# An MLP on products of split parts, and normalisations and expert weighting as two-input operations

## The chip, the core and the metric

The kernel runs on one core of a Trainium2 chip. The metric is the device time of one execution in microseconds; a version is run several times and its median is taken. The engines are PE (TensorE), DVE (VectorE), ACT (ScalarE), POOL (GpSimd) and the DMA queues of SP and ACT.

## The reference

A transformer block with self attention, cross attention and an MLP, then a router with three experts over evidence from the context, for 32 sequences of 128 tokens with 128 channels, all in float32. Cut to what matters:

```python
# B=32 sequences, N=128 tokens, H=128; S=128 tokens of context; 16 heads of 8; MLP = 512; E = 3 experts of 256
def L0(x, c, context, ...):
    shift_a, scale_a, gate_a, shift_m, scale_m, gate_m = split(silu(c) @ W_mod + b_mod, 6)
    x = x + gate_a * (attention(modulate(ln(x), shift_a, scale_a)) @ W_proj + b_proj)      # self
    x = x + attention(ln(x) @ W_qc + b_qc, ln(context) @ W_kvc + b_kvc) @ W_cproj + b_cproj  # cross
    x_norm2 = modulate(ln(x), shift_m, scale_m)            # ln(x) * (1 + scale_m) + shift_m
    h = gelu(x_norm2 @ W_mlp1 + b_mlp1)                    # [.., 512]
    return x + gate_m * (h @ W_mlp2 + b_mlp2)
def L1(x, anchor, bank, ...):                              # bank = the context
    nx = ln(x) * gamma + beta
    evidence = softmax((nx @ Wq) @ (bank @ Wk).T / sqrt(H)) @ (bank @ Wv)
    combined = concat(nx, evidence, anchor)
    p = softmax(combined @ router_W + router_b)            # 3 experts
    routed = sum_e p_e * (silu(combined @ e_w1[e] + e_b1[e]) @ e_w2[e] + e_b2[e])
    g = sigmoid(silu(combined @ gate_w1 + gate_b1) @ gate_w2 + gate_b2)
    return x + g * (routed @ out_w + out_b)
```

## The kernel before, in words

The 32 sequences are 8 groups (`NG`) of 4 (`GB`), a group's tile is 128 x 512 (`GT`). The first 325 us are attention, in rounds of an order written out by hand: `round_steps` gives each step a time, and every engine goes through the same list and does its own part of each step; `attention_events` turns it into events. The last attention round also derives the router's weights (`derive`) and, on POOL, takes the router's weights apart into a high part, rounded to the format fp32r, and a rest (`split_weights`, which calls `split`, lines 656 to 661). Its first steps of the MLP are the events of round `NG`, then `between_cores` and `rest_of_groups` go on: each engine runs the steps of `MLP_STEPS` for i = 2, 3, 4 alone and for i = 5, 6, 7 mixed with the first steps of the router (`ROUTER_STEPS`), then the router's groups.

One group g of the MLP goes through these steps, and an entry `(name, lag, k)` does it for group i + lag:

- `stats` (L806 to L812 on DVE, L648 and L650 on POOL): mean and variance, then the inverse deviation `rstd` as a power on POOL. `norm` (L820, DVE): `(x - mean) * rstd` into `m_XN`, four instructions of 128 x 128, each with mean and rstd as one value per token.
- `xt` (PE, L975): four transposes of `m_XN` into PSUM. `xt_read` (ACT, L725): four reads with scale and shift into `m_XT`.
- `first` (PE, L939): W_mlp1's chunk k (of 4) times `m_XT`, in float32; the trace shows two matmul records for one such product. `gelu` (ACT, L713) reads the bank into `m_H[:, k]`.
- `second` (PE): W_mlp2's chunk k times `m_H[:, k]`, all four into one bank, for the group before. `gate` (DVE, L835) reads that bank into `YT`; `turn_back` (PE) transposes it back, and DVE adds it to `X` (L841).

Engines are strictly in order: what stands behind a wait in an engine's list waits too. `m_XT`, `m_XN` and each chunk of `m_H` have one buffer, the FIRST and SECOND banks two each. In the router, `hidden` already works with split parts: for each weight and each input it makes three products (high by high, high by rest, rest by high) with `r_WNS`, `r_US`, `r_NXS`, `r_EVS`; the inputs are taken apart by `split` on POOL. `expert` (DVE, L914 to L920) adds biases (`r_T`) and weights three experts into `r_R`.

## Time and profile before

| | |
|---|---|
| median of 3 runs | 578.65 us (576.69 to 580.65) |
| the profiled execution | 576.7 us, of which its span is 574.9 us |
| PE, PEld busy | 541.4 us (94%), 382.1 us (66%) |
| DVE, ACT, POOL busy | 424.2 us (74%), 384.0 us (67%), 271.3 us (47%) |
| mean granted clock of TensorE | 0.993 of 2.4 GHz |

All times of rows are of the profiled execution, counted from the start of its span. A row of a timeline gives start, length, engine, line, operation, output and inputs (buffer numbers left out; PS is PSUM) and count; behind it, in brackets, the idle time of the engine and what ended it. PE is the matmul part of TensorE and PEld its loading of weights. The ends of matmuls are modelled, so that the distance from one start to the next is the surer price.

### The profile page before, as it was taken

What the parts mean: (1) busy time and instruction counts of PE and PEld (TensorE: products, weight loads), DVE (VectorE), ACT (ScalarE), POOL (GpSimd) and SP (SyncE); (2) the same over time, 40 slices, a digit from 0 to 9 for tenths busy, and PEclk for the clock granted to TensorE, in tenths of its full rate; (3) what the DMA queues carried; (4) which work ended last, traced back from release to release, by engine and by line L of the source; (5) the groups of instructions that cost most, each with busy time, mean ns of one, the idle gap of its engine ahead of it and who ended that gap; (6) DMA issues with size and microseconds to landing.
All of it is one profiled execution on the core that took longest, in us unless ns stands there. A gap on an engine that the chain in (4) does not pass through costs nothing.

```text
span 574.9 us, 16422 instructions
## 1 busy us (share of the span) xinstructions
PE 541.4 (94%) x6177; PEld 382.1 (66%) x6177; DVE 424.2 (74%) x1255; ACT 384.0 (67%) x897; POOL 271.3 (47%) x294
## 2 busy tenths in 40 slices
PE   6988999999999999999999989997999999999995
PEld 5745665566666666666667534454788788788895
DVE  4788988888899798989787534556586786786565
ACT  6547687677777778787776655464754854854862
POOL 5638769399494878888903210124034034034000
PEclk9999999899999999999999899999999999999999
DMA  4765656344153543344400010000001001000000
GB/s 130 159 170 132 176 149 150 78 114 124 45 133 91 133 117 96 89 107 117 114 5 3 2 36 0 2 1 19 0 20 39 20 19 36 18 18 20 19 20 18
DMA packets 48716, 39.38 MB, mean 69 GB/s; under 512 B 6241, under 2 KB 48002, under 8 KB 48642
## 3 DMA queue, kind: packets, MB, share of 16 engines
q1 hardware_dynamic: 46568, 34.62, 23.3%
q10 hardware_dynamic: 2074, 3.77, 2.3%
q8 instruction: 47, 0.77, 0.6%
q14 instruction: 27, 0.22, 0.1%
HBM read 10.06 MB, written 2.10 MB: 21 GB/s over the span
## 4 chain that ended last, share of the span: by engine, by line
PE 64%; DVE 11%; POOL 7%; DMA 5%; ACT 4%; SPq 4%; issue 3%; ACTq 0%; DVEq 0%; POOLq 0%
PE PS L939 35%; PE PS L1808 6%; PE PS L1774 5%; PE PS L975 3%; SPq L1322 3%; PE PS L1860 3%; DVE NM L1590 3%; PE PS L1872 3%; DMA Qs<-MT 2%; PE PS L1792 2%; PE PS L1830 2%; PE PS L1865 2%; DMA Ks<-Kp 1%; POOL rstd L1368 1%; POOL rest L1399 1%
## 5 line engine op out<-in xcount | busy, mean ns | idle before, releaser
L1590 DVE TENSOR_REDUCE NM<-PS 128x4 f32<-128x512 f32 x256 | 163.4, 682 | 30.9 <-PE PS L1774 30.3
L1476 ACT ACTIVATE PR<-PS 128x512 f32<-128x512 f32 x256 | 139.7, 600 | 28.1 <-PE PS L1792 27.4
L1774 PEld LDWEIGHTS PS<-Ks,Qs 64*128 64x128 bf16 x1024 | 57.3, 94 | 53.4 <-DVE NM L1590 29.3
L1774 PE MATMUL PS<-Ks,Qs 64*128 64x128 bf16 x1024 | 83.6, 218 | 5.8 <-DVE NM L1590 3.8
L1792 PE MATMUL PS<-Qs,Ks 64*128 64x128 bf16 x1024 | 83.7, 219 | 4.5 <-DMA Qs<-MT 3.9
L1808 PE MATMUL PS<-PR,Va 128*32 128x128 f32 x2048 | 83.1, 280 | 0.0
L733 ACT ACTIVATE r_HID<-PS,ANC 128x128 f32<-128x128 f32 x224 | 63.0, 380 | 19.4 <-PE PS L939 19.3
L648 POOL TENSOR_TENSOR m_veps<-m_mv,m_eps 128x4 f32<-128x4 f32 x16 | 3.2, 201 | 143.0 <-DVE m_mv L812 143.0
L1792 PEld LDWEIGHTS PS<-Qs,Ks 64*128 64x128 bf16 x1024 | 57.1, 94 | 8.3 <-DMA Qs<-MT 4.4
L1808 PEld LDWEIGHTS PS<-PR,Va 128*32 128x32 f32 x2048 | 48.5, 109 | 20.9 <-issue 6.0
L939 PE MATMUL PS<-r_NXS,r_WNS 128*128 128x512 f32 x168 | 53.1, 424 | 0.0
L939 PE MATMUL PS<-WO,r_HID 128*128 128x128 f32 x384 | 47.7, 278 | 0.2
L939 PE MATMUL PS<-r_EVS,r_US 128*128 128x512 f32 x168 | 47.7, 392 | 0.0
L939 PEld LDWEIGHTS PS<-WO,r_HID 128*128 128x128 f32 x384 | 44.6, 192 | 1.6 <-DVE r_T L914 1.3
L1860 PE MATMUL PS<-XT,W 128*128 128x512 f32 x64 | 34.9, 633 | 1.9 <-ACT XT L1512 1.4
L939 PEld LDWEIGHTS PS<-r_EVS,r_US 128*128 128x128 f32 x168 | 31.5, 188 | 7.2
L939 PEld LDWEIGHTS PS<-r_NXS,r_WNS 128*128 128x128 f32 x168 | 29.5, 189 | 7.7 <-issue 3.4
L713 ACT ACTIVATE m_H<-PS,V 128x512 f32<-128x512 f32 x32 | 21.3, 692 | 19.8 <-PE PS L939 19.8
L939 PE MATMUL PS<-m_XT,W 128*128 128x512 f32 x64 | 32.0, 600 | 0.3 <-ACT m_XT L725 0.3
L939 PE MATMUL PS<-m_H,W 128*128 128x512 f32 x64 | 31.5, 592 | 0.0
L762 ACT ACTIVATE r_GTH<-r_GS 128x512 f32<-128x512 f32 x8 | 5.0, 631 | 38.7 <-DVE r_GS L907 38.7
L659 POOL TENSOR_TENSOR r_EVS<-r_EV,zeros 128x512 fp32r<-128x512 f32 x8 | 8.3, 1039 | 47.5 <-DVE r_EV L888 47.5
(197 smaller groups left out, 1103.6 us busy)
## 6 DMA issues: line engine op xcount, KB each, us to landing
Qs<-Qp SPq DMA_DIRECT2D x96, 128.0 KB
Ks<-Kp SPq DMA_DIRECT2D x90, 128.0 KB
CTXG<-in_ctx SPq DMA_DIRECT2D x8, 256.0 KB, 3.6
r_CTX<-in_ctx SPq DMA_DIRECT2D x8, 256.0 KB, 2.9
out<-X SPq DMA_DIRECT2D x8, 256.0 KB, 2.3
X<-in_x SPq DMA_DIRECT2D x7, 256.0 KB, 4.4
W<-in_weights ACTq DMA_DIRECT2D x2, 855.0 KB
Qs<-MT SPq DMA_DIRECT2D x62, 8.0 KB
```

What stands on the lines that cost most here:

```text
L713: nc.scalar.activation(H[:, k, :], FIRST_BANK[k % 2][:, :], ACT.Gelu_apprx_tanh, bias=vec("bmlp1", k))\
L733: last = nc.scalar.activation(HID[:, k, b * P:(b + 1) * P], HIDDEN_BANK[k % 3][:, b * P:(b + 1) * P], ACT.Silu, bias=ANC[:, k, bass.ds(g * ...
L939: return nc.tensor.matmul(to, lhsT, rhs, start=start, stop=stop)
L975: last = nc.tensor.transpose(bank[:, b * P:(b + 1) * P], source(b), ident[:, :])
L1322: sp.dma_start(to, source).then_inc(stacked[k], 16)
L1476: nc.scalar.activation(PR[:, u, :], T_BANK[u % 2][:, :], ACT.Exp, scale=SCALE)\
L1590: nc.vector.tensor_reduce(out=NM[:, c.b // 2, c.second, u // 2, u % 2 * 4:u % 2 * 4 + 4, 0], in_=S_BANK[score_bank(c, u)[0]][:, :].rearran ...
L1774: last = nc.tensor.matmul(S_BANK[bank][:, j * P:(j + 1) * P], Qs[c.stack][rows, lo + j, cols], Ks[c.stack][rows, lo + j, cols], start=True ...
L1792: last = nc.tensor.matmul(T_BANK[u % 2][:, j * P:(j + 1) * P], Ks[c.stack][rows, lo + j, cols], Qs[c.stack][rows, lo + j, cols], start=Tru ...
L1808: last = nc.tensor.matmul(O_BANK[p.turn][TW * j:TW * j + TW, at:at + P], Va[c.mem][:, c.b, 4 * (u // 2) + j, u % 2 * TW // 2:u % 2 * TW // ...
L1860: last = nc.tensor.matmul(PS[fill_bank(name, g)][:, :], w(WEIGHT[name[0]][kind]), source(name, g)[:, :], start=True, stop=True)
L1872: last = nc.tensor.matmul(GROUP_BANK[:, :], w(("proj", "cproj")[KIND[name]]), OgT[KIND[name]][:, :], start=True, stop=True)
```

## The change

- *Products of the MLP.* `m_W1S` and `m_W2S` hold the high part and the rest of W_mlp1 and W_mlp2; POOL makes them in the last attention round with `split` (the same two operations as for the router's weights), behind a wait for the score steps that used the memory under them. The stacks `Qs` and `Ks` are laid out in another order for that.
- *The input.* A new step `xt_parts` on DVE copies `m_XT` into the high part of `m_XTS` (two buffers) and subtracts it from `m_XT` for the rest. `xt_read` now comes right behind `xt` in `MLP_STEPS`, with `xt_parts` behind it.
- *The hidden values.* Behind each gelu, ACT waits for it and copies `m_H[:, k]` into the high part of `m_HS`; POOL subtracts for the rest. `second` waits for the rest.
- *PE* makes three products of split parts for each `first` and each `second`, where it made one in float32. It also waits for the weights' parts.
- *Two-input forms.* `normalise` (MLP and router) becomes `scalar_tensor_tensor` with rstd as a broadcast second tensor; the first expert's weighting (`r_R`, L917) becomes `tensor_tensor` with a broadcast second tensor.
- Four semaphores of the attention are used again, with their counts carried on.

Hunk headers keep the line numbers; context is cut. `split` is the function at line 656.

```diff
@@ -243,7 +243,7 @@
...
                  + fill_steps(31.0, "mlp_xt", 0, (0, 31.1))
-                 + [(t, "split", "weights", k, 0) for k, t in enumerate((2.5, 6.0, 22.5, 24.5))]
+                 + [(t, "split", "weights", k, 0) for k, t in enumerate((2.5, 6.0, 9.0, 12.0, 22.5, 24.5))]
                  + mlp_steps(21.2, "stats", 0) + mlp_steps(23.4, "norm", 0)
@@ -256,7 +256,7 @@
...
                  + mlp_steps(8.43, "second", 0, 3) + mlp_steps(8.44, "norm", 3) + mlp_steps(8.45, "first", 1, 2)
-                 + mlp_steps(8.46, "first", 1, 3) + mlp_steps(8.47, "xt_read", 2) + mlp_steps(8.48, "gelu", 1, 2)
+                 + mlp_steps(8.46, "first", 1, 3) + mlp_steps(8.35, "xt_read", 2) + mlp_steps(8.36, "xt_parts", 2) + mlp_steps(5.11, "xt_parts", 1) + mlp_steps(8.48, "gelu", 1, 2)
                  + mlp_steps(8.49, "gelu", 1, 3) + mlp_steps(8.5, "gate", 0))
@@ -381,9 +381,9 @@
...
 MLP_STEPS = (
-    ("stats", 2, 0), ("xt", 1, 0),
+    ("stats", 2, 0), ("xt", 1, 0), ("xt_read", 1, 0), ("xt_parts", 1, 0),
     ("first", 0, 0), ("second", -1, 0), ("first", 0, 1), ("second", -1, 1),
-    ("turn_back", -2, 0), ("norm", 2, 0), ("first", 0, 2), ("first", 0, 3), ("xt_read", 1, 0),
+    ("turn_back", -2, 0), ("norm", 2, 0), ("first", 0, 2), ("first", 0, 3),
     ("second", -1, 2), ("gelu", 0, 2), ("second", -1, 3), ("gelu", 0, 3), ("gate", -1, 0),
@@ -458,7 +458,8 @@
...
 def mlp_and_router(nc, stack, X, V, ctxin, w, vec, rows1, condT, mod, gbm, half, zeros, YT, ident, PS, load_w2, out,
-                   bank_filled, bank_read, max_done, exp_done, o_normed, o_stored):
+                   bank_filled, bank_read, shifted_done, max_done, exp_done, o_normed, o_stored,
+                   high_ready, low_ready):
@@ -530,6 +531,10 @@
...
     D = rb("r_D", [P, GT])
+    W1S = rb("m_W1S", [P, 2, 4 * P], F32R)
+    W2S = rb("m_W2S", [P, 2, 4 * P], F32R)
+    XTS = [rb(f"m_XTS{k}", [P, 2, GT], F32R) for k in range(2)]
+    HS = rb("m_HS", [P, 2, 4, GT], F32R)
@@ -553,6 +558,8 @@
...
     bank_filled["mlp_xt"], bank_read["mlp_xt"] = xt_turned, xt_read
+
+    xt_high, xt_split, h_high, h_split = (high_ready["k0"], low_ready["k0"], high_ready["q0"], low_ready["q0"])
     masked = sem("masked")
@@ -652,6 +659,9 @@
...
                 inverse_deviation(0, g)
+            elif name == "first" and k < 2 or name == "gelu":
+                pool.wait_ge(h_high, 4 * g + (NG + k + 1))
+                nc.gpsimd.tensor_tensor(HS[:, 1, k, :], H[:, k, :], HS[:, 0, k, :], ALU.subtract).then_inc(h_split, 1)
@@ -679,8 +689,13 @@
...
                 pool.wait_ge(load_w2, 80)
-            elif k > 1:
-                pool.wait_ge(bank_read["derive"], DERIVED.index(("u_low", "u_high")[k - 2]) + 1)
+            elif k in (2, 3):
+
+                pool.wait_ge(shifted_done, 16 * (2 * NG - 2))
+                to, source = ((W1S, w("mlp1")), (W2S, w("mlp2")))[k - 2]
+                return split(to, source, (weights_high, k + 1), weights_split)
+            elif k > 3:
+                pool.wait_ge(bank_read["derive"], DERIVED.index(("u_low", "u_high")[k - 4]) + 1)
             to, source = (WNS, w("e_nx", lo, hi - lo)) if k < 2 else (US, U[:, lo:hi])
@@ -709,9 +724,13 @@
...
             if later(g):
-                act.wait_ge(second_done, 4 * g + (k - 3))
+                act.wait_ge(h_split, 4 * g + (NG + k - 3))
             nc.scalar.activation(H[:, k, :], FIRST_BANK[k % 2][:, :], ACT.Gelu_apprx_tanh, bias=vec("bmlp1", k))\
                 .then_inc(gelu_done, 1)
+            act.wait_ge(gelu_done, 4 * g + (k + 1))
+            if later(g):
+                act.wait_ge(second_done, 4 * g + (k - 3))
+            nc.scalar.activation(HS[:, 0, k, :], H[:, k, :], ACT.Copy).then_inc(h_high, 1)
@@ -719,7 +738,7 @@
...
                 if later(g):
-                    act.wait_ge(first_done, 4 * g)
+                    act.wait_ge(xt_split, g + NG)
                 for b in range(GB):
@@ -817,8 +836,8 @@
...
             for b in range(GB):
-                last = nc.vector.tensor_scalar(to[:, b * P:(b + 1) * P], x_batch(g, b), mv[:, s, b, 0:1],
-                                               rstd[:, s, b:b + 1], ALU.subtract, ALU.mult)
+                last = nc.vector.scalar_tensor_tensor(to[:, b * P:(b + 1) * P], x_batch(g, b), mv[:, s, b, 0:1],
+                                                      rstd[:, s, b:b + 1].to_broadcast([P, P]), ALU.subtract, ALU.mult)
             last.then_inc(d_norm[s], 1)
@@ -826,6 +845,17 @@
...
                 normalise(0, g, XN, xt_turned)
+            elif name == "xt_parts":
+                dve.wait_ge(xt_read, g + 1)
+                if g > 1:
+                    dve.wait_ge(first_done, 4 * (g - 1))
+                elif g == 1:
+                    dve.wait_ge(exp_done, 4 * NCORE)
+                else:
+                    dve.wait_ge(shifted_done, 16 * (2 * NG - 2))
+                nc.vector.tensor_copy(XTS[par][:, 0, :], XT[:, :]).then_inc(xt_high, 1)
+                dve.wait_ge(xt_high, g + (NG + 1))
+                nc.vector.tensor_tensor(XTS[par][:, 1, :], XT[:, :], XTS[par][:, 0, :], ALU.subtract).then_inc(xt_split, 1)
             elif name == "gate":
@@ -914,7 +944,7 @@
...
                 dve.wait_ge(expert_read, GB * g + (b + 1))
-                nc.vector.tensor_scalar(R[:, b, :], t[:, 0:P], RP[:, b, 0:1], None, ALU.mult).then_inc(routed, 1)
+                nc.vector.tensor_tensor(R[:, b, :], t[:, 0:P], RP[:, b, 0:1].to_broadcast([P, P]), ALU.mult).then_inc(routed, 1)
                 for e in range(1, NE):
@@ -985,17 +1015,23 @@
...
                     pe.wait_ge(exp_done, 4 * NCORE)
+                    pe.wait_ge(weights_split, 4)
                 if k == 0:
-                    pe.wait_ge(xt_read, g + 1)
+                    pe.wait_ge(xt_split, g + (NG + 1))
                 if k > 1 or later(g):
                     pe.wait_ge(gelu_done, 4 * g + (k - 1))
-                product(FIRST_BANK[k % 2][:, :], w("mlp1", k * P, P), XT[:, :]).then_inc(first_done, 1)
+                chunk = slice(k * P, (k + 1) * P)
+                product(FIRST_BANK[k % 2][:, :], W1S[:, 0, chunk], XTS[par][:, 0, :], True, False)
+                product(FIRST_BANK[k % 2][:, :], W1S[:, 0, chunk], XTS[par][:, 1, :], False, False)
+                product(FIRST_BANK[k % 2][:, :], W1S[:, 1, chunk], XTS[par][:, 0, :], False, True).then_inc(first_done, 1)
             elif name == "second":
...
                     pe.wait_ge(x_added, g - 1)
-                pe.wait_ge(gelu_done, 4 * g + (k + 1))
-                product(SECOND_BANK[par][:, :], w("mlp2", k * P, P), H[:, k, :], start=k == 0, stop=k == 3)\
-                    .then_inc(second_done, 1)
+                pe.wait_ge(h_split, 4 * g + (NG + k + 1))
+                chunk = slice(k * P, (k + 1) * P)
+                product(SECOND_BANK[par][:, :], W2S[:, 0, chunk], HS[:, 0, k, :], k == 0, False)
+                product(SECOND_BANK[par][:, :], W2S[:, 0, chunk], HS[:, 1, k, :], False, False)
+                product(SECOND_BANK[par][:, :], W2S[:, 1, chunk], HS[:, 0, k, :], False, k == 3).then_inc(second_done, 1)
             elif name == "turn_back":
@@ -1088,7 +1124,7 @@
...
-            pe.wait_ge(weights_split, 2 * -(-NHC * P // GT))
+            pe.wait_ge(weights_split, 2 * -(-NHC * P // GT) + 2)
             pe.wait_ge(xt_read, NG)
@@ -1192,7 +1228,7 @@
...
             nc, stack, X, V, ctxin, w, vec, rows1, condT, mod, gbm, half, zeros, YT, ident, PS, load_w2, out,
-            bank_filled, bank_read, max_done, exp_done, o_normed, o_stored)
+            bank_filled, bank_read, shifted_done, max_done, exp_done, o_normed, o_stored, high_ready, low_ready)
@@ -1205,8 +1241,6 @@
...
         rest = sb("rest", [P, 2, GT])
-        Qs = [sb(f"Qs{k}", [P, NJ, GT], BF16) for k in range(STACKS)]
-        Ks = [sb(f"Ks{k}", [P, NJ, GT], BF16) for k in range(STACKS)]
         zrow = sb("zrow", [32, GT], BF16)
@@ -1217,6 +1251,9 @@
...
         On = sb("On", [P, 2, 2 * P])
+        Qs, Ks = [None] * STACKS, [None] * STACKS
+        for k in (1, 0, 2):
+            Qs[k], Ks[k] = (sb(f"{what}s{k}", [P, NJ, GT], BF16) for what in "QK")
         OgT = [sb(f"OgT{k}", [P, GT]) for k in range(2)]
@@ -1369,6 +1406,8 @@
...
                     extra["split"](ev[2])
+                elif ev[:2] == ("read", "mlp_xt"):
+                    extra["mlp"]("xt_parts", 0, 0, 0, 0)
                 elif ev[:2] == ("init", "third"):
@@ -1716,6 +1755,8 @@
...
                     extra["derive"](DERIVED[ev[2]], ev[3])
+                elif ev[:2] == ("read", "mlp_xt"):
+                    extra["mlp"]("xt_parts", 0, 0, 0, 0)
                 elif name == "read" and ev[1] in ("yt_s", "yt_c"):
```

## Rows read from the trace of the kernel before

**Rows 1.** Chain of waits, 325 to 404 us: share of each line.

```profile
by line: PE PS L939 69.0%; PE PS L975 11.2%; ACT m_XT L725 5.5%; issue 3.3%; ACT m_H L713 2.0%; ACT r_E L744 1.9%; ACT L744 1.6%; PE PS L1872 1.4%; ACT L713 1.2%; DVE r_EV L888 0.9%; ACT r_CTXT L738 0.6%; PE PS L1830 0.6%; PE PS L1876 0.6%;
```

**Rows 2.** Windows: length, busy of PE, PEld, DVE, ACT, POOL; clock, DMA, GB/s.

```profile
325.80:342.15 16.35, 13.71 (x44) 6.59 (x44) 7.76 (x38) 9.75 (x20) 2.41 (x4) 1.00 0.12 33
...
350.35:358.50 8.15, 8.12 (x24) 3.77 (x25) 4.30 (x18) 4.03 (x9) 1.20 (x2) 1.00 0.00 0
...
366.65:375.90 9.25, 9.24 (x30) 4.70 (x31) 6.16 (x29) 5.20 (x11) 2.16 (x4) 1.00 0.00 1
```

**Rows 3.** Timeline of PE in the MLP: start, us, what, count.

```profile
363.03 1.88 PE L939 MATMUL PS<-m_XT,W 128*128 128x512 f32 x4
364.75 1.88 PE L939 MATMUL PS<-m_H,W 128*128 128x512 f32 x4
```

**Rows 4.** Timeline of PE in the router, products of split parts.

```profile
553.84 0.85 PE L939 MATMUL PS<-r_NXS,r_WNS 128*128 128x512 f32 x3
554.52 0.84 PE L939 MATMUL PS<-r_EVS,r_US 128*128 128x512 f32 x3
```

**Rows 5.** ACT: timeline of one group; last, the Tanh's line (ns min/median/max).

```profile
352.98 0.69 ACT L713 ACTIVATE m_H<-PS,V 128x512 f32<-128x512 f32 x1 [1.62 <-PE PS L939]
...
356.86 1.50 ACT L725 ACTIVATE m_XT<-PS,mod 128x128 f32<-128x128 f32 x4 [1.47 <-PE PS L939]
...
L762 ACT ACTIVATE r_GTH<-r_GS x8: 629/630/632, 424.3 to 566.0; 128x512 f32<-128x512 f32 x8
```

**Rows 6.** Timeline of DVE in the same group.

```profile
350.36 1.37 DVE L835 TENSOR_SCALAR YT<-PS,mod,gbm 128x128 f32<-128x128 f32 x4 [1.72 <-PE PS L939]
351.64 0.86 DVE L806 BATCH_NORM_STATS2 m_stat<-X 128x6 f32<-128x128 f32 x4
...
352.61 0.37 DVE L812 BATCH_NORM_AGGREGATE m_mv<-m_stat 128x2 f32<-128x6 f32 x4
355.08 0.69 DVE L841 TENSOR_TENSOR X<-PS,X 128x512 f32<-128x512 f32 x1 [2.09 <-PE PS L975]
355.69 1.11 DVE L820 TENSOR_SCALAR m_XN<-X,m_mv,m_rstd 128x128 f32<-128x128 f32 x4
```

**Rows 7.** Timelines of POOL and DVE, 311 to 317 us.

```profile
311.25 0.20 POOL L648 TENSOR_TENSOR m_veps<-m_mv,m_eps 128x4 f32<-128x4 f32 x1 [23.71 <-DVE m_mv L812]
...
312.52 1.04 POOL L659 TENSOR_TENSOR r_US<-U,zeros 128x512 fp32r<-128x512 f32 x1
313.63 1.27 POOL L661 TENSOR_TENSOR r_US<-U,r_US 128x512 fp32r<-128x512 f32 x1
...
312.58 4.27 DVE L820 TENSOR_SCALAR m_XN<-X,m_mv,m_rstd 128x128 f32<-128x128 f32 x4 [1.41 <-POOL m_rstd L650]
```

**Rows 8.** Timelines of POOL and DVE at 16 and at 400 us.

```profile
15.86 1.22 POOL L1403 TENSOR_TENSOR Kp<-rest,Kp 128x512 bf16<-128x512 f32 x1
...
16.09 1.53 DVE L1715 TENSOR_TENSOR Qp<-rest,Qp 128x512 bf16<-128x512 f32 x1
...
399.28 1.04 POOL L659 TENSOR_TENSOR r_NXS<-r_NX,zeros 128x512 fp32r<-128x512 f32 x1
...
399.79 0.56 DVE L900 TENSOR_TENSOR r_LS<-r_LG,r_lmax 128x12 f32<-128x12 f32 x1
400.27 1.36 DVE L835 TENSOR_SCALAR YT<-PS,mod,gbm 128x128 f32<-128x128 f32 x4
```

**Rows 9.** r_R: line of its scalar form (ns), timeline of DVE, waits of PE.

```profile
L917 DVE TENSOR_SCALAR r_R<-r_T,r_RP x32: 285/286/1028, 421.0 to 569.6; 128x128 f32<-128x128 f32 x32
...
443.51 0.74 DVE L920 SCALAR_TENSOR_TENSOR r_R<-r_T,r_RP,r_R 128x128 f32<-128x128 f32 x2
...
PEld PS L939 <- DVE r_T L914: 1.3, 6, 0.3
```

**Rows 10.** Windows around an idle PE, columns as in Rows 2.

```profile
316.60:317.50 0.90, 0.07 (x2) 0.00 (x0) 0.90 (x4) 0.90 (x3) 0.17 (x1) 0.87 0.00 0
317.50:318.50 1.00, 0.97 (x1) 0.50 (x2) 0.96 (x7) 0.26 (x1) 0.00 (x0) 0.50 0.00 0
```

## The prediction

> **What bounds the kernel now.** I read the windows by stretch first, to find the stage that the change touches: the MLP of eight groups runs from 325.8 to 404.1 us, and the router behind it. The chain of waits inside that stage [rows 1] is 69% matrix products of line 939, 11% transposes, and only 5.5% ACT's read of XT: TensorE sets the pace. The reader should see in [rows 2] that one pure MLP group takes 8.15 us with PE busy 8.12 of them, while DVE works 4.30, ACT 4.03 and POOL 1.21. PE's own timeline [rows 3] gives the price of a product: four matmuls are issued in 1.72 us (363.03 to 364.75), so one product (two records) holds PE for 0.86; eight products are 6.88, the two sets of four transposes about 0.44 each. The products of split parts that the router already has [rows 4] start 0.68 us apart for three (553.84 to 554.52), so a product costs 0.68.
>
> **The change, part by part.**
> (a) Products. 8 groups x 8 products x (0.86 - 0.68) = 11.5 us less on PE; per group 1.44. That is the whole possible gain, and only as long as PE stays last.
> (b) ACT. Each gelu (0.69) gets a Copy of 128x512 behind it, which waits for the gelu itself. The trace has no such SBUF-to-SBUF copy; the nearest row is the Tanh from SBUF, 0.63, so I take 0.60 (bounds 0.53, if its start overlaps the work before it, and 0.69). ACT per group: XT read 1.38 net of overlap, four times 0.69+0.03+0.60 = 5.28, sum 6.7 [rows 5]; a copy also waits for the `second` product of the group before, about 0.4 once per group: 7.1. So ACT becomes the bound near 7.1 us if nothing else waits.
> (c) POOL. Four subtracts per group. The nearest row, the low half of `split`, is 1.27 [rows 7], so 5.1 a group, beside the inverse deviation, 1.27 (311.25 to 312.52): 6.3.
> (d) DVE. Now [rows 6]: gate 1.37, statistics 1.34 (351.64 to the end of the averages, 352.61 + 0.37), x addition 0.69, normalise 1.11, 4.30 with little else. Added: copy 0.42 (bounds 0.35 and 0.69; estimates from half and all of the 0.69 that one 128x512 operation takes) and subtract 0.69. Normalise as a two-input form: 4 x 0.32 = 1.3, because two of the two-input r_R operations take 0.74 together, and the scalar form 0.286 [rows 9]; about 6.0 in all without waits.
> (e) The lock between DVE and POOL, which decides the case. At 312.58 four normalise operations took 4.27 us instead of 1.11 [rows 7]: POOL was busy without a pause, and each DVE operation came through only as one POOL operation ended, one for one, and POOL's own rows follow each other with next to no gap (312.52 + 1.04, then 313.63). The question is whether the two-input form escapes this. [Rows 8] say no: the TENSOR_TENSOR of 16.09, both inputs in SBUF, took 1.53 against the 0.69 of [rows 6]; POOL's operation ended at 17.08 and the DVE one 0.54 later, so it did all its work behind POOL's. The one of 399.79, with 12 elements a partition, took 0.56 and ended 0.03 behind POOL's (399.28 + 1.04). Operations of DVE that read PSUM are not held (YT at 400.27: four in 1.36, as at 350.36, with POOL at work beside it). So the change puts 5.1 us of POOL reads per group beside six DVE operations that must wait for them: copy, subtract, and four normalises.
>
> Walk through one locked group, time 0 where the last normalise of group g+1 ends: transposes, ACT starts at 0.72; XT read to 2.1; gelu 2.8; copy 3.4; POOL could subtract at 3.5. DVE meanwhile did the gate (to 1.3) and statistics (to 2.6), so POOL, in order, is at the inverse deviation until 4.0, and the subtracts start there. DVE: copy and subtract of XT from 2.6 to 3.8 (4.6 if the inverse deviation's pow on POOL holds it), x addition to 4.4 or more: the first normalise meets the first subtract. All four pass behind the four subtracts: 4.0 + 4 x 1.3 + 0.15 = 9.4, and 9.8 with the end of the XT subtract behind the pow. If one of the four slips in ahead: 8.0. So a group takes 8.0 to 9.8 against 8.15; I take the middle, 8.98.
>
> The sum, in stages.
> *Start* (325.8 to 342.15): `first` of group 0 waits for copy and subtract, +1.1; cheaper products and the earlier XT read give back about 3; the normalise of group 3 behind four subtracts of group 1 is +4.1; the XT subtract or one normalise more behind a POOL operation is +0.3 to +2.6. Together +2.5 to +4.8, I take +3.7.
> *Three pure groups* to 366.65 (the iterations that start at 342.15, 350.35 and 358.50): -0.4 to +5.0, I take +2.5.
> *Mixed stage*, 366.65 to 404.1, of which the first iteration took 9.25: PE saves up to 0.18 x 24 = -4.3. Against it, the two router normalises queue behind subtracts (+1.5 to +4), of ACT's 8 copies (4.8) around two loads of a table and the exps I let half show (+2.4), and the last `second` has copy 0.60 and subtract 1.27 in front of it, perhaps a router split of 2.3 as well (+1.9 to +4.2). Together +1.5 to +6.3; these waits overlap in part, so I take +3.2.
> *Router*: its r_R operation waits for POOL in some groups (up to 1.03 against 0.29) and will go on waiting; PE's waits for r_T total 1.3 us [rows 9], so nothing above that could be won. In the last group, four times 0.07 (half of 0.74, less 0.286, rounded down) lie on the path: +0.3.
> *Splits of W1 and W2*, two at about 2.3: free, they fall into POOL's idle time of 23.71 us before 311.25 [rows 7]; without that cover they would cost 4.6. Their wait counts 224 of the 256 shifted score steps, which are complete as the last attention round starts. PE's wait for them is met long before 325. The reuse of semaphores and the new order of buffers cost nothing that a row shows. The stall at 312.58 stays: the same operations, +0.07.
> Sum: 3.7 + 2.5 + 3.2 + 0.3 = +9.7 us (bounds +3.9 and +16.4). The profiled execution was 576.7, 1.8 more than its span, and the median of the three runs 1.95 above it: 578.65 + 9.7 = 588.4.
>
> The Trainium skill bears on (e): its page "SBUF — State Buffer", section "Who interferes with whom", says that a Vector instruction with two SBUF inputs also contends with a GpSimd instruction that reads SBUF, that the pair is held for the whole instruction, and that whoever comes first blocks the other. The waits of DVE agree (1.53 and 0.56 above). By the second half POOL would lose DVE's data time as well, an estimate of 0.27 + 0.53 a group from that page's rule; the trace shows POOL's next operation starting 0.07 behind its last at 313.63 although DVE had just come through, so the sum has no such term; by the rule it would be up to 6 us more.
>
> **The rivals.**
> *No lock* (the other sign): the form with a broadcast second operand does not wait, or POOL's pauses let it through. Then ACT sets 7.1 us per group: start -1.9, three groups -3.2, mixed stage -0.4, in all -5.5: 573.1. For it: the work of every engine is under 7.1. Against it: [rows 8]. If even ACT's copies were hidden, PE's 11.5 would be the limit, 567. It decides from the point where the four normalises take under about 2.5 us.
> *Mild lock*: the phases of DVE and POOL settle so that one or two normalises wait, -2 to +4: 579.5. A group of 8.0 is this side's end.
> *The clock*: in a locked group PE is idle about 3 us in 9.8. An idle PE of 0.86 us at 316.6 was followed by a granted clock of 0.50 in the next stretch [rows 10], the lower level of 1.2 GHz, while in 325.80 to 342.15 PE was idle for 2.64 us in all and the clock stayed at 1.00 [rows 2]. At the lower level the eight products need 10.9 us, more than the group. If that happens in half of the groups, +8 on top of the forecast: 596.
>
> **How the numbers follow.** About 1% is what a measurement of this kernel can tell. Chances: forecast (+3.9 to +16.4) 0.58, clock 0.10, mild lock 0.15, no lock 0.17. Faster by over 1% needs -5.8: the better half of no lock, 0.09. Within 1%: the rest of it, mild lock, and the forecast's lowest edge, 0.28. Slower: 0.63. The range leaves out the best of no lock and the worst of the clock: 573 to 598.
>
> **What would show it.** Right: the product's starts 0.68 apart; normalise m_XN over 3 us per group, each operation ending as a POOL subtract ends; PE waiting for m_XN's transposes; a group of 8 to 10 us; the MLP 7 to 13 us longer. Wrong: normalise at 1.3 us per group, ACT near full and a group near 7.1 (no lock), or a PEclk row under 9 in that stage (clock). The forecast is too high if the XT copy and subtract regularly come before the subtracts of POOL, and too low if POOL is delayed in its turn.

## The result, and the profile after

Three executions of the changed kernel took 588.1, 588.5 and 590.9 us, beside a median of 579.2 us (576.7 to 580.7) for the kernel before: the ratio on record is 1.0214, 95% interval 1.0156 to 1.0272, some 12 us; the two medians alone give 9.3 us. A fourth execution was in a slow state (1223.8 us, at a granted clock of 1.000, without a trace that could say why) and is not in these numbers; with it the median would be 589.7. The profiled execution took 588.5 us, its span 586.7, where that of the kernel before had 574.9.

The page of the kernel after, first the busy times, the slices of PE and its clock, and the chain that ended last:

```profile
PE 536.3 (91%) x6241; PEld 398.3 (68%) x6241; DVE 452.8 (77%) x1271; ACT 403.2 (69%) x929; POOL 319.6 (54%) x330
...
PE   7988999999999999999998776876999999999995
...
PEclk9999999999999999999999989787999999999998
...
PE 55%; DVE 18%; POOL 10%; issue 5%; DMA 5%; SPq 4%; ACT 3%; ACTq 0%; DVEq 0%; POOLq 0%
...
L664 POOL TENSOR_TENSOR m_HS<-m_H,m_HS 128x512 fp32r<-128x512 f32 x32 | 41.4, 1312 | 18.2 <-ACT m_HS L733 18.1
```

PE has holes in slices 22 to 28 (308 to 411 us), nearly all of them in the MLP, and its clock row falls to 7 and 8 there. The chain inside that stage (318 to 416 us) answers to [rows 1]: products of the MLP were 69% of it; now line 969 has under a third, and the normalisation, a line that did not appear before, has 13.5%:

```profile
by line: PE PS L969 31.8%; DVE m_XN L839 13.5%; issue 10.9%; PE PS L1005 8.2%; POOL m_HS L664 5.1%; DVE r_XN L839 3.1%; POOL m_rstd L657 2.6%; DVE m_XTS L858 2.4%; DVE YT L865 2.4%; DVE m_stat L825 1.6%; DVE m_XTS L856 1.5%; ACT m_H L728 1.
```

The windows between the transposes of successive groups have the columns of [rows 2], whose pure group was 8.15 us with PE busy for 8.12:

```profile
330.47:340.75 10.28, 5.22 (x27) 4.16 (x27) 8.18 (x17) 6.34 (x12) 8.04 (x7) 0.97 0.17 51
340.75:348.77 8.02, 7.92 (x33) 6.33 (x33) 6.14 (x21) 5.42 (x11) 3.95 (x4) 0.82 0.00 0
348.77:358.70 9.93, 6.79 (x32) 5.10 (x32) 9.60 (x21) 7.38 (x14) 9.50 (x8) 1.00 0.01 3
358.70:368.39 9.69, 6.62 (x33) 5.21 (x33) 9.23 (x21) 6.36 (x12) 6.85 (x6) 0.95 0.00 0
368.39:378.92 10.53, 10.53 (x38) 8.31 (x39) 6.96 (x25) 6.58 (x13) 3.93 (x4) 0.72 0.00 1
```

Two kinds of group take turns. In three of the five PE works 5.2 to 6.8 us and DVE 8.2 to 9.6: DVE is last. In the other two (8.02 and 10.53) PE is busy nearly to the end, at a mean clock of 0.82 and 0.72 of 2.4 GHz, that is, for a part of the time at the lower level of 1.2. The timeline of the third window shows what DVE does:

```profile
351.84 0.69 DVE L858 TENSOR_TENSOR m_XTS<-m_XT,m_XTS 128x512 fp32r<-128x512 f32 x1
351.94 1.46 POOL L657 TENSOR_TENSOR m_rstd<-m_veps,half 128x4 f32<-128x4 f32 x1
...
353.38 5.13 POOL L664 TENSOR_TENSOR m_HS<-m_H,m_HS 128x512 fp32r<-128x512 f32 x4
353.44 5.21 DVE L839 SCALAR_TENSOR_TENSOR m_XN<-X,m_mv,m_rstd 128x128 f32<-128x128 f32 x4
...
358.70 0.66 PE L1005 MATMUL PS<-ident,m_XN 128*128 128x128 f32 x4 [3.14 <-DVE m_XN L839]
```

Four normalisations took 5.21 us, as four subtractions beside them took 5.13; each of the four ended 0.15 us behind the end of a subtraction, and PE stood idle for 3.14 us until the last was done. In [rows 7] this was a single stall at 312.58. Now it comes in full in three more of the eight groups (5.16, 5.21 and 5.12 us); in the other four the normalisations took 1.1 to 2.2 us, so that none or one of them waited.

To see where the time went I cut every execution at the same four marks: the first transpose of group 0 (line 1005), those of groups 3 and 6, and the first product of the router's hidden layer. The first column is the time of the first mark. Start, pure groups, mixed stage and router are the distances between them and to the end, in us; the kernels of the experiments are in the same table.

```
kernel          attention  start   pure  mixed  router  | ratio to before, 95%
before             323.3    18.9   24.5   37.5   170.8  |
after              318.2    22.5   27.6   47.5   170.8  | 1.0214 1.0156-1.0272
before_layout      322.7    18.9   24.5   37.5   170.9  | 0.9961 0.9933-0.9989
one_input          323.4    22.2   27.4   44.8   170.4  | 1.0194 1.0137-1.0252
pe_filler          318.1    22.5   27.6   43.2   170.8  | 1.0185 1.0153-1.0216
rest_dve           322.2    24.8   23.2   43.7   170.8  | 1.0150 1.0100-1.0201
halves             320.6    22.9   23.8   43.1   170.8  | 1.0140 1.0106-1.0174
second_only        320.5    18.8   24.2   44.4   170.8  | 1.0087 1.0056-1.0117
norm_in_two        316.2    21.0   24.4   44.7   170.8  | 1.0081 1.0050-1.0113
no_rest            318.8    18.5   21.7   41.2   170.8  | 0.9971 0.9942-1.0001
first_load         321.1    23.3   27.2   42.6   171.2  | 1.0203 1.0151-1.0256
first_only         322.1    16.4   21.3   35.9   171.2  | 0.9871 0.9843-0.9899
half_second        322.0    17.7   20.5   38.1   170.9  | 0.9868 0.9824-0.9912
first_one          318.7    16.4   21.3   35.9   170.8  | 0.9825 0.9785-0.9865
```

Between the two profiled executions the MLP grew by 16.8 us (3.6 + 3.2 + 10.0), the router by nothing, and the attention stage, in which no instruction was to become faster, was 5.1 us shorter.

### The profile page after: what moved, and what is told of

Same layout as the page of the kernel before. It is cut to its first block, busy times and chain, and to the rows that moved or that the text cites. A ratio compares the mean times of both kernels' runs of the same rounds, so it can differ in the third digit from the quotient of the medians.

```text
span 586.7 us, 16671 instructions
## 1 busy us (share of the span) xinstructions
PE 536.3 (91%) x6241; PEld 398.3 (68%) x6241; DVE 452.8 (77%) x1271; ACT 403.2 (69%) x929; POOL 319.6 (54%) x330
## 4 chain that ended last, share of the span: by engine, by line
PE 55%; DVE 18%; POOL 10%; issue 5%; DMA 5%; SPq 4%; ACT 3%; ACTq 0%; DVEq 0%; POOLq 0%
PE PS L969 27%; PE PS L1849 6%; PE PS L1815 5%; DVE m_XN L839 3%; PE PS L1005 3%; PE PS L1901 3%; DVE NM L1629 3%; SPq L1359 3%; DMA Qs<-MT 2%; PE PS L1833 2%; PE PS L1913 2%; PE PS L1871 2%; PE PS L1906 2%; DVE r_T L944 1%; DMA Ks<-Kp 1%
## 5 line engine op out<-in xcount | busy, mean ns | idle before, releaser
L664 POOL TENSOR_TENSOR m_HS<-m_H,m_HS 128x512 fp32r<-128x512 f32 x32 | 41.4, 1312 | 18.2 <-ACT m_HS L733 18.1
L969 PE MATMUL PS<-m_XTS,m_W1S 128*128 128x512 f32 x96 | 31.8, 458 | 1.5 <-DVE m_XTS L858 1.5
L1402 POOL TENSOR_TENSOR veps<-mv,eps 128x4 f32<-128x4 f32 x24 | 4.9, 203 | 47.0 <-DVE mv L1694 47.0
```

Source lines behind the costliest of these rows:

```text
L664: nc.gpsimd.tensor_tensor(HS[:, 1, k, :], H[:, k, :], HS[:, 0, k, :], ALU.subtract).then_inc(h_split, 1)
L969: return nc.tensor.matmul(to, lhsT, rhs, start=start, stop=stop)
```

## The experiments

**1. The subtractions left out.** no_rest keeps POOL's subtraction for group 0 alone:

```diff
-            elif name == "first" and k < 2 or name == "gelu":
+            elif g == 0 and (name == "first" and k < 2 or name == "gelu"):
                 pool.wait_ge(h_high, 4 * g + (NG + k + 1))
...
-                pe.wait_ge(h_split, 4 * g + (NG + k + 1))
+                pe.wait_ge(h_high if g else h_split, 4 * g + (NG + k + 1))
```

> The changed kernel, with POOL's subtraction of the rests of the gelu outputs left out from the second group on: the middle product of each second MLP product then reads the rests of group 0, so its part of the output is wrong by the size of a rest. TensorE's 24 products a group, ACT's copies and DVE's parts stay. Theory A (the subtractions, in turn with DVE's normalisations and parts, set the length of a group): the groups fall from about 10 us to 7.2 to 7.8 us, and the time to 572 to 577 us. Rival B (ACT's copies, or the longer chain gelu, copy, second product): the copies remain, groups of over 9 us, 586 us or more. Rival C (TensorE at half its clock in this stretch costs the time): nothing here changes what the clock depends on in a known way, so 586 to 590 us with the same low clock.

It took 574.5 us beside 575.7: its ratio is 2.4% under the changed kernel's, some 14 us. That is in theory A's range, and not in that of B or C. But the cut also takes the subtraction out of the chain from the gelu to the second product, and out of what the next gelu waits for. And the clock did not stay as it was: its mean was 0.979 to 0.992 here against 0.973 to 0.979, so a part of the 14 us can be the clock's. It is no clear gain over the kernel before (the interval reaches 1.0001): the three pure groups took 6.4, 7.6 and 7.6 us, and in the last two PE, though it has less work, waits again:

```profile
351.34:358.96 7.62, 6.97 (x33) 5.26 (x32) 5.35 (x20) 6.36 (x13) 1.21 (x2) 1.00 0.00 0
```

**2. One of the two products at a time.** first_only takes the second product back to fp32, with the gelu output as before and nothing on ACT or POOL; second_only does the opposite. The core of first_only:

```diff
-                nc.gpsimd.tensor_tensor(HS[:, 1, k, :], H[:, k, :], HS[:, 0, k, :], ALU.subtract).then_inc(h_split, 1)
...
-            nc.scalar.activation(HS[:, 0, k, :], H[:, k, :], ACT.Copy).then_inc(h_high, 1)
...
-                product(SECOND_BANK[par][:, :], W2S[:, 0, chunk], HS[:, 0, k, :], k == 0, False)
-                product(SECOND_BANK[par][:, :], W2S[:, 0, chunk], HS[:, 1, k, :], False, False)
-                product(SECOND_BANK[par][:, :], W2S[:, 1, chunk], HS[:, 0, k, :], False, k == 3).then_inc(second_done, 1)
+                product(SECOND_BANK[par][:, :], w("mlp2", k * P, P), H[:, k, :], start=k == 0, stop=k == 3)\
+                    .then_inc(second_done, 1)
```

> The changed kernel, with the second MLP product back to fp32 from the gelu output: no copies on ACT, no subtractions on POOL; the first product still of split parts. Theory A: TensorE saves 4 x (0.86 - 0.68) = 0.7 us in each of 8 groups against the kernel before, and nothing waits for POOL; the start, where the parts have to be made before the first product, costs some 1 to 2 us: 573 to 577 us. Rival D (the longer chain from transpose over ACT and two DVE operations to the first product costs more than the products save, whatever POOL does): 580 to 585 us.

> The changed kernel, with the first MLP product back to fp32 from the transposed normalised x: no parts on DVE; the second product still of split parts, with ACT's copies and POOL's subtractions. Theory A: the four normalisations still go in turn with the four subtractions, but the two operations for the parts and their waits are gone: groups of 8.2 to 9.2 us, 580 to 585 us. Rival D (the chain for the parts costs the time): 574 to 578 us. Rival B (ACT's copies and the chain behind the gelu): 586 us or more.

568.8 us and 581.0 us: the first split alone is 1.3% faster than the kernel before, 4 us better than theory A's range had it; the second alone is 0.9% slower, within theory A's range, though its pure groups (8.4, 7.7 and 8.2 us) are at or under the foot of the 8.2 to 9.2 expected. The window of a pure group of first_only has PE busy to the end again:

```profile
352.64:359.74 7.10, 7.10 (x29) 4.51 (x28) 5.33 (x20) 4.05 (x9) 1.75 (x2) 1.00 0.00 0
```

That is 1.05 us under the 8.15 of before, where the four cheaper products give only 0.72; nearly all of the other 0.33 stands at the two sets of four transposes, which took 0.58 and 0.44 us from their start to the next start before, and 0.36 each here; why they cost less is not shown. Rival D falls: the longer chain to the first product is hidden.

**3. The load alone.** first_load is first_only with POOL's four subtractions a group put back, of constant data into a tile that nobody reads; nobody waits for them (the edit is shown against first_only):

```diff
+            elif name == "first" and k < 2 or name == "gelu":
+                pool.wait_ge(gelu_done, 4 * g + (k + 1))
+                nc.gpsimd.tensor_tensor(HS[:, 1, k, :], w("mlp2"), W2S[:, 0, :], ALU.subtract)
```

> The kernel first_only (only the first product of split parts; 7.10 us a group, TensorE without a gap) with a load on POOL that nobody needs: at each gelu one subtraction of 128x512 of constant data into a tile that nobody reads, four a group. No wait of any other engine is added, and ACT and TensorE do what they did. Theory A (POOL's subtractions hold up DVE's operations with two SBUF inputs one for one): DVE's 5.3 us a group grow by 2 to 4 us of waits, past TensorE's 7.1: groups of 8 to 9.5 us and 575 to 586 us. Rival B (POOL costs only through the chain gelu, copy, rest, second product): 567 to 571 us, as without the load.

587.5 us beside first_only's 568.8: +18.6 us, for work that no instruction waits for, a little more than theory A's range had. This is the cleanest of the runs: no engine waits for the new work. The one thing that could queue behind it is POOL's own inverse deviation, and DVE's wait for that grew by 0.9 us only (the last numbers of the two rows below). So what is left is what POOL's reads do to DVE, and what follows from that; the lower clock follows as well, in this profile with up to 5.5 of the 18.6 us (an estimate: half of the time that PE worked at 1.2 GHz in the MLP; none in first_only). The groups of lines of DVE in 323 to 400 us, first_only and then first_load:

```profile
L832 DVE SCALAR_TENSOR_TENSOR m_XN<-X,m_mv,m_rstd 128x128 f32<-128x128 f32 x28 | 7.9, 346 | 0.9 <-POOL m_rstd L657 0.9
```

```profile
L835 DVE SCALAR_TENSOR_TENSOR m_XN<-X,m_mv,m_rstd 128x128 f32<-128x128 f32 x28 | 21.6, 831 | 1.8 <-POOL m_rstd L657 1.8
```

and the same group of the kernel after:

```profile
L839 DVE SCALAR_TENSOR_TENSOR m_XN<-X,m_mv,m_rstd 128x128 f32<-128x128 f32 x24 | 21.6, 957 | 1.2 <-POOL m_rstd L657 1.1
```

In first_load 28 x (831 - 346) ns = 13.6 us are waits inside the normalisations, and in the changed kernel 24 x (957 - 346) ns = 14.7 us. PE's idle time in the MLP grew by 13.7 us from first_only to first_load.

**4. The size of what is waited for.** halves cuts each subtraction into two of 256 columns; norm_in_two does the four normalisations of a group of the MLP as two operations of 512 columns, the router's as before.

```diff
+                for lo in range(0, GT, GT // 2):
+                    part = slice(lo, lo + GT // 2)
+                    last = nc.gpsimd.tensor_tensor(HS[:, 1, k, part], H[:, k, part], HS[:, 0, k, part], ALU.subtract)
+                last.then_inc(h_split, 1)
```

> The changed kernel, with each subtraction of 128x512 on POOL cut into two of 128x256. Theory A (a DVE operation with two inputs in SBUF gets through at the end of a POOL operation, one for one): a locked normalisation takes some 0.75 us in place of 1.3, so four of them 3 us in place of 5.2; a group becomes 1 to 2 us shorter, the time 577 to 584 us. If POOL's fixed cost eats the gain (two halves take over 1.7 us in place of 1.3), 585 to 590 us. Rivals B and C: no difference, 588 to 591 us; or longer, if only POOL's total matters.

```diff
+                nc.vector.tensor_tensor(t, x, mv[:, 0, :, 0:1].to_broadcast([P, GB, P]), ALU.subtract)\
+                    .then_inc(x_centred, 1)
+                dve.wait_ge(x_centred, g + 2)
+                nc.vector.tensor_tensor(t, t, rstd[:, 0, :].unsqueeze(2).to_broadcast([P, GB, P]), ALU.mult)\
+                    .then_inc(d_norm[0], 1)
```

> The changed kernel, with the four normalisations of 128x128 a group in two operations of 128x512 (x minus the mean, spread over the columns; then times the reciprocal deviation): about 1.4 us of DVE without waits, as before, but two operations that can meet a subtraction of POOL where there were four. Theory A (one wait for each operation, whatever its size): two locked operations take up to 2 x 1.35 us in place of 4 x 1.3, groups 1 to 2.5 us shorter: 574 to 581 us. If a longer operation waits longer, in proportion to its columns, no gain: 585 to 589 us.

584.0 us (the top of the expected range) and 581.3 us (just above it). The timelines, first of halves, then of norm_in_two:

```profile
356.44 3.70 POOL L666 TENSOR_TENSOR m_HS<-m_H,m_HS 128x256 fp32r<-128x256 f32 x5
356.50 3.05 DVE L842 SCALAR_TENSOR_TENSOR m_XN<-X,m_mv,m_rstd 128x128 f32<-128x128 f32 x4 [0.26 <-POOL m_rstd L657]
```

```profile
349.99 5.92 POOL L665 TENSOR_TENSOR m_HS<-m_H,m_HS 128x512 fp32r<-128x512 f32 x4
350.20 1.64 DVE L842 TENSOR_TENSOR m_XN<-X,m_mv 128x512 f32<-128x512 f32 x1
351.87 1.65 DVE L845 TENSOR_TENSOR m_XN<-m_XN,m_rstd 128x512 f32<-128x512 f32 x1
```

Behind POOL operations of half the size four normalisations take 3.05 us, not 5.21; as two operations they take 3.3. So a DVE operation waits once, for the POOL operation under way, at both of the sizes tried. The three pure groups fall by 3.9 and 3.3 us in sum. What the prediction left out shows in the second timeline: beside DVE's 512-column operations POOL's four subtractions take 5.92 us, not 5.13, because two of them take 1.73 each and not 1.3. POOL waits in its turn.

**5. The two-input forms undone.** one_input has tensor_scalar again for normalisation and first weighting.

```diff
-                last = nc.vector.scalar_tensor_tensor(to[:, b * P:(b + 1) * P], x_batch(g, b), mv[:, s, b, 0:1],
-                                                      rstd[:, s, b:b + 1].to_broadcast([P, P]), ALU.subtract, ALU.mult)
+                last = nc.vector.tensor_scalar(to[:, b * P:(b + 1) * P], x_batch(g, b), mv[:, s, b, 0:1],
+                                               rstd[:, s, b:b + 1], ALU.subtract, ALU.mult)
```

> The changed kernel, with the two-input forms undone: normalisations and the first expert weighting again as tensor_scalar. Theory A as the prediction has it (the old form waits for POOL's subtractions just as the new one does; without one beside it it takes 0.28 us in place of 0.34): 585 to 590 us. Rival E (only the new form waits): 573 to 580 us.

589.2 us, ratio 1.0194: no difference from the changed kernel that the intervals can tell. Rival E falls, since the old form waits as the new one does:

```profile
358.48 5.01 DVE L839 TENSOR_SCALAR m_XN<-X,m_mv,m_rstd 128x128 f32<-128x128 f32 x4 [0.19 <-POOL m_rstd L657]
```

**6. The rests on DVE.** rest_dve moves the four subtractions to DVE, at the same places of the order.

```diff
+        def h_rest(g, k):
+            dve.wait_ge(h_high, 4 * g + (NG + k + 1))
+            nc.vector.tensor_tensor(HS[:, 1, k, :], H[:, k, :], HS[:, 0, k, :], ALU.subtract).then_inc(h_split, 1)
...
+            if name == "first" and k < 2 or name == "gelu":
+                h_rest(g, k)
```

> The changed kernel, with the rests of the gelu outputs computed by DVE in place of POOL, at the same places of the order. DVE has 5.35 + 4 x 0.69 = 8.1 us of work a group and no operation of POOL beside it but the small ones. Theory A (the price is the meeting of the two engines, not the work): 8.1 to 9 us a group, 577 to 584 us, less than with POOL although DVE does more. Rival B (the chain behind the gelu sets the group; DVE now also stands waiting for ACT's copies): 588 us or more.

586.4 us: a miss for theory A's number, 2 us above its range. Its pure groups (8.2, 7.4 and 7.6 us) are as short as expected or shorter, and 4.4 us shorter in sum than with POOL. Two of them:

```profile
347.02:355.18 8.16, 6.57 (x32) 5.21 (x33) 7.81 (x25) 6.98 (x14) 1.75 (x2) 1.00 0.00 0
355.18:362.60 7.42, 6.57 (x32) 5.18 (x32) 7.35 (x25) 5.90 (x12) 1.68 (x2) 1.00 0.01 3
```

But the start (24.8 us) is longer than in any other kernel, and the mixed stage 6.2 us longer than before. In both TensorE worked for a part of the time at 1.2 GHz (mean clock 0.86 and 0.88, against 1.00 before), which makes up to 3.5 and 5.2 us of them (an estimate: length times what is missing from 1). In the whole time the two ways can't be told apart, as the intervals of 1.0150 and 1.0214 overlap: only the pure groups show that meeting POOL is dearer than DVE's extra work.

**7. The clock.** pe_filler gives TensorE ten spare products in each of groups 3 to 7, ahead of the wait in which it was idle.

```diff
+                if g > 2:
+                    for _ in range(10):
+                        product(SCORE_BANK[1][:, :], W1S[:, 0, 0:P], W1S[:, 0, :])
                 pe.wait_ge(d_norm[0], g + 1)
```

> The changed kernel, with ten further products of split weights (128x512, 0.23 us each, 2.3 us in all) ahead of the wait for the normalised x, in groups 3 to 7, into a PSUM bank that nobody reads: there TensorE stood idle for 3 to 5 us in most of these groups. In the profile of the changed kernel TensorE was granted half the clock for some 20 us of the MLP stage, and two stretches with TensorE busy throughout lay in it (8.0 us at 0.82 with 7.92 busy, 10.5 us at 0.72 with 10.53 busy). Theory H (idle time made by the waits is followed by half clock, and that costs a part of the time, 3 to 8 us): with less idle time the clock stays up and the time is 581 to 587 us although TensorE does more. Theory A alone (what DVE waits for POOL sets the groups, and the clock costs nothing beside it): 588 to 596 us, since the fillers take up to 5 x 2.3 us and are hidden only where TensorE waited.

588.1 us, ratio 1.0185, at the lowest edge of theory A's range and just above theory H's. The mean granted clock of its six executions is 0.983 to 0.993, that of the changed kernel 0.973 to 0.979: it rose in all of them, and the time fell by 0.3%, less than the intervals can tell. In the profiled execution, the fastest of the six, two middle groups are:

```profile
350.88:359.54 8.66, 8.66 (x43) 7.16 (x42) 6.45 (x21) 6.36 (x12) 6.35 (x7) 1.00 0.00 1
359.54:368.21 8.67, 8.67 (x43) 7.16 (x42) 6.52 (x21) 6.36 (x12) 6.35 (x7) 1.00 0.00 0
```

Its three pure groups are as long in sum as those of the changed kernel (27.6 us), with 2.3 us more work of PE in each; its mixed stage is 4.2 us shorter, with 2.3 us of fillers in it. This is no clean test of the clock, for two reasons. PE is now busy throughout the pure groups, so the fillers are in part on the path. And they moved the meetings: in the two groups where the normalisations had taken 5.21 and 5.12 us they took 2.29 and 2.28. What the clock alone costs stays open.

**8. The memory layout.** before_layout is the kernel before with the buffers in the new places, the new tiles unused.

```diff
+    HS = rb("m_HS", [P, 2, 4, GT], F32R)
...
+        Qs, Ks = [None] * STACKS, [None] * STACKS
+        for k in (1, 0, 2):
+            Qs[k], Ks[k] = (sb(f"{what}s{k}", [P, NJ, GT], BF16) for what in "QK")
```

> The kernel before, with the memory layout of the changed one alone: the stacked Q and K buffers allocated late and in the order 1, 0, 2, the new tiles allocated and never written. In the profiled executions the changed kernel had come to its first MLP transposes 5.1 us earlier than the kernel before. Theory F (the layout makes the attention stage shorter): 571 to 574 us, 2 to 5 us under the kernel before. Theory G (chance of single executions: attention waits on DMA and on stretches of half clock that differ from one execution to the next): within 1 us of the kernel before.

574.2 us beside 576.6, ratio 0.9961 (0.9933 to 0.9989): 2.2 us less, the lower end of theory F's 2 to 5. In its profile the MLP is as in the kernel before to 0.1 us, and it is reached 0.6 us earlier. Executions with the new layout reached the MLP at 316.2 to 323.4 us, and the clock goes with that: the five profiled executions that had no stretch at 1.2 GHz ahead of the MLP (after, pe_filler, norm_in_two, no_rest, first_one) reached it at 316.2 to 318.8 us, the nine that had one to three of them, the kernel before with two, at 320.5 to 323.4. So some 3 of the 5.1 us are the clock of single executions: PE was busy for 302.3 us ahead of the MLP before, and for 299.2 after.

**9. What can be had.** first_one is first_only with the one-input forms; half_second adds to it the second split for k = 0 and 1, rests by DVE behind the normalisations:

```diff
+            if name == "first" and k > 1:
+                h_rest(g, k - 2)
...
+                if k < 2:
+                    pe.wait_ge(h_split, 2 * g + (NG + k + 1))
+                    product(SECOND_BANK[par][:, :], W2S[:, 0, chunk], HS[:, 0, k, :], k == 0, False)
+                    product(SECOND_BANK[par][:, :], W2S[:, 0, chunk], HS[:, 1, k, :], False, False)
+                    product(SECOND_BANK[par][:, :], W2S[:, 1, chunk], HS[:, 0, k, :], False, False).then_inc(second_done, 1)
+                    return
```

> The kernel first_only (568.8 us) with the one-input forms of normalisation and first expert weighting. With no subtractions on POOL, TensorE bounds the groups (7.10 us of 7.10), so the normalisations give nothing there; the first weighting is off or on the chain of the router once for each expert step, at most 8 x 4 x 0.06 us = 2 us, and of that 0.4 us by the distance from the first hidden product to the end in two profiles: 567.5 to 569 us.

> The kernel first_one with two of the four second products of each group (k = 0 and 1) of split parts as well: high parts by ACT, rests by DVE, not POOL, behind the normalisations. TensorE saves 2 x 0.18 us a group (7.10 to 6.74); DVE goes from 5.1 to 6.5 us, ACT from 4.05 to 5.3. By these sums 0.36 us x 8 less: 565 to 567 us. If the chains of waits bound the group by then, 568 to 575 us; the kernel no_rest, with all second products split and nothing on POOL, took 7.6 us a group where TensorE needed 6.4, which speaks for that.

first_one took 566.8 us, ratio 0.9825 (0.9785 to 0.9865). It is the fastest of all, 1.75% under the kernel before, 3.8% under the changed one, and 0.7 us under its expected range; its interval overlaps that of first_only, so the one-input forms may give nothing. half_second took 569.3 us, which is the second of its two expectations (568 to 575): its three pure groups gain 0.9 us in sum, and it gives back 1.4 us at the start and 2.2 in the mixed stage, some 1.5 of these with the clock (0.96 there).

## Why the prediction was right, and where it was not

The predicted 588.4 us and the measured 588.1 to 590.9 differ by less than the interval. The mechanism was the one forecast. The number has luck in it: the waits were taken a little too high, the clock was left out of the sum, and a shorter attention stage hid a part of what was missing.

- **(a) Products.** Three products of split parts take 0.68 us as forecast. TensorE's saving is real only where nothing else is last: first_only gets it, and more.
- **(b) ACT.** A copy takes 0.63 us (forecast 0.60, bounds 0.53 to 0.69). As a bound of 7.1 us a group, ACT is not borne out: no_rest, with all copies, had a pure group of 6.4 us, with PE busy throughout, and two of 7.6.
- **(c), (d) POOL and DVE.** 1.31 us a subtraction (1.27), 0.39 to 0.43 for the copy of XT (0.42), 0.69 for its rest, 0.34 for a normalisation (0.32): right. DVE's whole work in a group without waits is 5.3 us (first_only), not "about 6.0".
- **(e) The lock.** Right, and shown by experiments 3 and 4: one wait a DVE operation, for the POOL operation under way; experiment 5 shows that both forms wait. The Trainium skill, page "SBUF — State Buffer", section "Who interferes with whom", has POOL wait as well. By the trace it does: POOL's pow took 1.46 us where DVE's subtraction of 512 columns had started 0.10 us before it, against 1.01 in no_rest (last section), and two of the subtractions beside norm_in_two's operations took 1.73 each against 1.3. That whoever comes first blocks the other, as the prediction has it from that section, the pow does not bear out (last section). The forecast's sum had no such term, on a row with 128-column operations, where it is small (5.13 us for four). Its upper estimate of 6 us from that page's rule did not come about here: the pow lost 0.45 us in three groups of the changed kernel and up to 0.15 in three more, a subtraction 0.03. The other direction, the pow holding DVE's rest of XT, which the 9.8 us at the top of its range for a group counted in, did not happen: in the pure groups that rest took its 0.69 us each time. (The 8.98 that it took for a group is also not the middle of 8.0 and 9.8, which is 8.9.)
- **Start** +3.6 (predicted +3.7, counted from the transposes, as its +1.1 for the wait of group 0 was). **Pure groups** +3.2 (+2.5). **Router** 0.0 (+0.3).
- **Mixed stage** +10.0, predicted +3.2 with bounds of +1.5 to +6.3. **This is the term that was mis-sized**, and what its sum lacked is work at the lower clock. The stage in the kernel before, in the changed kernel, in no_rest and in pe_filler:

```profile
366.66:404.14 37.48, 34.56 (x136) 19.33 (x137) 22.17 (x80) 20.13 (x45) 10.51 (x12) 1.00 0.03 8
```

```profile
368.39:415.86 47.47, 37.84 (x164) 29.63 (x165) 29.56 (x84) 27.00 (x56) 26.36 (x24) 0.83 0.02 6
```

```profile
358.96:400.13 41.17, 34.02 (x166) 26.92 (x164) 24.55 (x84) 29.51 (x60) 10.52 (x12) 0.92 0.03 8
```

```profile
368.21:411.45 43.24, 34.63 (x176) 27.33 (x174) 26.95 (x77) 26.67 (x56) 26.36 (x25) 0.96 0.02 7
```

  PE's idle time grew from 2.9 to 9.6 us, by 6.7; the prediction's +3.2 and its 4.3 of cheaper products stand for 7.5 of waits. But PE's busy time, which should have fallen by 4.3, rose by 3.3: the 7.6 us between are products at 1.2 GHz (mean clock 0.83, against 1.00 before). Over the whole MLP the idle time grew by 18.4 us where the forecast needs 9.4 + 11.5 = 20.9. PE's busy time went from 74.8 to 73.2 us, where the cheaper products should have taken away 11.5: the lower clock took 9 to 10 us that the sum didn't have. Whether all of them were on the path is not shown: with a faster PE a part would have become waiting.

  The forecast waits are all in the trace. A router normalisation behind subtractions left PE idle for 4.29 us:

```profile
381.90 4.39 POOL L664 TENSOR_TENSOR m_HS<-m_H,m_HS 128x512 fp32r<-128x512 f32 x3
...
383.83 3.14 DVE L839 SCALAR_TENSOR_TENSOR r_XN<-X,m_mv,m_rstd 128x128 f32<-128x128 f32 x4
...
387.02 0.66 PE L1005 MATMUL PS<-ident,r_XN 128*128 128x128 f32 x4 [4.29 <-DVE r_XN L839]
...
399.25 1.22 PE L969 MATMUL PS<-r_CTXT,A 128*128 128x512 f32 x1 [3.11 <-ACT r_CTXT L757]
```

  The last row is the part that the prediction let "half show, +2.4": ACT works in order, and the router's reads now stand behind gelus, copies and table loads. The cuts separate the two. With the copies and second split parts but without any lock (no_rest 41.2, first_only 35.9) the mixed stage is 5.3 us longer: 3.9 us more of idle PE and some 3.5 at 1.2 GHz, less 2.2 for cheaper products. The subtractions make a further 3.6 to 6.3 us (one_input 44.8 and after 47.5, over 41.2); of the 6.3, 2.5 are idle time of PE and 3.8 are products at the lower clock. The waits of no_rest name ACT:

```profile
PE PS L969 <- ACT r_CTXT L757: 3.9, 1, 3.9
```

- **Attention** was taken as unchanged ("the new order of buffers cost nothing that a row shows"). It was 5.1 us shorter in the profile, some 3 of it by the clock of the two executions (experiment 8). If the ratio of before_layout is the layout's alone, the change of the MLP costs 1.0214 / 0.9961 = 1.0254, some 14.6 us (an estimate) against the 9.7 forecast.
- **The rivals.** No lock did not happen. Of mild lock the changed kernel has single groups, those where the normalisations took 2.0 to 2.2 us. The clock did happen, as a companion: TensorE was at 1.2 GHz in stretches between 340 and 405 us (windows at 0.82 and 0.72 above). The prediction had it at 0.10 and +8 us on top, and named a PEclk row under 9 in this stage as a sign that it would be wrong; that row reads 8, 9, 7, 8, 7. Another of its signs, the MLP 7 to 13 us longer, was missed as well, with 16.8. What the clock costs lies between nothing and the 9 to 10 us above, and experiment 7 doesn't narrow it.

## What to carry to other kernels

Before work is moved to a second engine, look which operations will run beside it, not only how full that engine is: here 5.2 us a group of POOL work in idle time cost DVE 14.7 us of waits, more than the 11.5 that TensorE was to save, and even unread dummy work cost 3.3%. Where such meetings can't be avoided, what counted in these runs is the number of the one engine's operations times the length of the other's: fewer, larger operations on the waiting side gave back 7.7 us of it (1.0214 to 1.0081), smaller ones on the other side 4.3 (to 1.0140). And split a change before judging it: the half whose parts were made by DVE alone was worth 1.3%, hidden under a sum of +2.1%. Look at the granted clock of a stage before its length is put down to waits: here PE's busy time in the mixed stage rose although its work had become less.

## What was unexpected

- The kernel with the new places of the Q and K buffers alone was 0.4% faster (interval 0.1 to 0.7%), with no instruction changed. Its mean granted clock was a little higher too (0.994 against 0.992); whether the places, or the clock by chance, made the difference was not tested.
- A POOL operation of four elements a partition (the pow) took 1.46 us when DVE's 512-column subtraction was ahead of it by 0.1 us. It waits even where it starts first: in this group of the changed kernel it began 0.34 us ahead of the subtraction and still ended 0.14 behind it, while the subtraction took its usual 0.69:

```profile
343.54 1.17 POOL L657 TENSOR_TENSOR m_rstd<-m_veps,half 128x4 f32<-128x4 f32 x1
...
343.88 0.69 DVE L858 TENSOR_TENSOR m_XTS<-m_XT,m_XTS 128x512 fp32r<-128x512 f32 x1
```

  In no_rest it began 0.81 us ahead, and neither waited:

```profile
346.97 1.01 POOL L657 TENSOR_TENSOR m_rstd<-m_veps,half 128x4 f32<-128x4 f32 x1
...
347.78 0.69 DVE L858 TENSOR_TENSOR m_XTS<-m_XT,m_XTS 128x512 fp32r<-128x512 f32 x1
```

- TensorE's stretches at 1.2 GHz in the MLP of the changed kernel each began in or behind idle time that another engine's waits had made (5.06, 3.07, 4.29 and 3.11 us); one idle time of 3.14 us, at 358.7, was not followed by one. Filling idle time with spare products raised the mean clock from 0.976 to 0.987 without a gain that could be told.
